# Two-part F32R queries and keys, two heads stacked in the halves of the TensorE array, and maxima units of two PSUM banks

## The chip, the cores and the metric

The kernel runs on one core of one Trainium2 chip. The metric is the device time of one execution in microseconds, from the first instruction to the last. It is given as the median of three runs. A profile of one more execution is read beside it. The core's engines are PE (TensorE, the matrix array), DVE (VectorE), ACT (ScalarE), POOL (GpSimd) and SP (SyncE, which here only issues transfers). Each works through its own stream of instructions in order, and they meet at semaphores.

## The reference

Two batches of 2048 tokens of 256 numbers pass one attention layer with 16 heads of 16 dimensions and then a feed-forward layer with eight experts and a shared one. Each is added to its input and normalised.

```python
q_mat = split_heads(x @ Wq.T + bq)
k_mat = split_heads(x @ Wv.T + bv)
v_mat = split_heads(x @ Wk.T + bk)
q_mat, k_mat = _xpos_rotate(q_mat, k_mat)      # rotation and a scale by position
scores = jnp.einsum('bhqd,bhkd->bhqk', q_mat, k_mat) / math.sqrt(DH * NUM_HEADS)
scores = jnp.where(causal[None, None], scores, -jnp.inf)
weights = jax.nn.softmax(scores, axis=-1)
inter = jnp.einsum('bhqk,bhkd->bhqd', weights, v_mat)
...
return inter @ Wo.T + bo
...
x = _layernorm(x + attention(x)); x = _layernorm(x + experts(x))   # top 2 of 8, and the shared one
```

All inputs are 32-bit floats.

## The kernel before

The work falls into three stages.

*Projection.* 32 tiles of 128 tokens. For each, PE forms queries, keys and values (`project`, L547 and L554, plain 32-bit), DVE adds the biases (L853, L857), POOL multiplies by cosine and, with neighbours swapped, by sine (L1106, L1115), DVE adds the two (L864). A query or key is then split into three bf16 parts whose sum keeps its precision: ACT rounds to part 0 (L751), DVE subtracts (L868), ACT rounds to part 1 (L755), DVE subtracts to part 2 (L873). PE transposes the twelve 128x128 pieces (`turn_parts`, L566), ACT copies them out (L762), and every four tiles SP stores them to a scratch tensor in device memory (L1158).

*Attention.* The 16 heads of two batches make eight groups of four heads. For a group SP loads a stack of queries and a stack of keys (`load_stack`, L1174): 96 partitions hold six products of parts (`Q_PARTS`, `K_PARTS`) times 16 dimensions, so that one product of 96 rows sums them. Three more rows hold ones on the key side and, on the query side, the negative row maximum in three bf16 parts (L1177, L1188). There are three pairs of stacks. The staging buffers of the projection are the memory of stack 1.

The maxima come first: for a block of 512 queries, PE forms scores with queries on the PSUM partitions (`max`, L584, after a product with the causal mask on the diagonal, L582), one bank of up to 512 columns a unit. Four banks take turns. DVE reduces each (L879). When a block's units are done, DVE makes the shift (`shift`, L887 to L901), PE transposes it (`shift_rows`, L596), ACT copies (L770), SP puts the rows into the stack. Then come the scores themselves, keys on the partitions (`score`, L616), in steps of one tile of 128 keys by one block of 512 queries for four heads. ACT takes the exponential (L779), POOL zeroes the masked triangle on diagonal tiles (L1126), and PE multiplies by the values with the four heads in four column tiles of 32 (`attend`, L633). A group has 40 steps: 28 of 512 columns and four each of 384, 256 and 128. Three banks take turns for scores, and a score waits for the exponential three places before (`score_ring`). PE and DVE turn and normalise a finished block of output (L645, L906, L909).

*Experts.* Products of F32R pairs (high and low part, L525 to L527), with ACT, DVE and POOL beside. This stage isn't touched.

One list, `plan.order`, sets every engine's order. Maxima units are produced by a generator, and `attend_all` draws from it at a pace: during the last steps of the projection two or three at each of three places, later after each score, by a debt (`owed`) that grows with the score's width and shrinks by the unit's cost. The maxima thus run ahead of the scores, by up to a group and more. `load_stack n + 2` is issued when group n starts, stacks 1 and 2 right after the projection. In group 7 preparatory work of the experts (output products, weight splitting) takes the maxima's place.

## Time and profile before

| | us |
|---|---|
| median of 3 runs (lowest, highest) | 1504.7 (1504.17, 1504.73) |
| the profiled execution, as a whole | 1507.14 |
| its span from first to last instruction | 1505.6 |
| PE busy in the span | 1369.6 |
| DVE busy | 1201.3 |
| ACT busy | 868.5 |
| POOL busy | 371.8 |
| mean granted TensorE clock | 0.967 of full |

A row of a timeline gives the start, the length and the instruction, `xN` for N of them in a run, and in brackets how long the engine was idle before and who released it. A matrix product's length reaches to its modelled end, while the next one may start long before; what a product costs in a dense stream is the distance between starts. PEld is the loading of weights. A 32-bit product is recorded as two passes.

### The profile page before, as it was taken

What the parts mean: (1) busy time and instruction counts of PE and PEld (TensorE: products, weight loads), DVE (VectorE), ACT (ScalarE), POOL (GpSimd) and SP (SyncE); (2) the same over time, 40 slices, a digit from 0 to 9 for tenths busy, and PEclk for the clock granted to TensorE, in tenths of its full rate; (3) what the DMA queues carried; (4) which work ended last, traced back from release to release, by engine and by line L of the source; (5) the groups of instructions that cost most, each with busy time, mean ns of one, the idle gap of its engine ahead of it and who ended that gap; (6) DMA issues with size and microseconds to landing.
All of it is one profiled execution on the core that took longest, in us unless ns stands there. A gap on an engine that the chain in (4) does not pass through costs nothing.

```text
span 1505.6 us, 23890 instructions
## 1 busy us (share of the span) xinstructions
PE 1369.6 (91%) x8656; PEld 707.3 (47%) x8656; DVE 1201.3 (80%) x2438; ACT 868.5 (58%) x1686; POOL 371.8 (25%) x708
## 2 busy tenths in 40 slices
PE   6677685799999999999999999998989999999997
PEld 3444331333333333333333333333436888888886
DVE  6998995598888888888888888887865677667766
ACT  2554343466776776777776776776764344434443
POOL 8775410111112112112112112112101322222222
PEclk9998978799999999999999999999989999999999
DMA  2338239103304205106006000002200000000000
GB/s 89 113 113 141 82 71 124 23 2 49 39 1 58 30 1 68 20 2 79 10 2 86 2 2 1 2 1 71 92 29 15 15 15 14 1 15 15 15 15 29
DMA packets 35589, 58.36 MB, mean 39 GB/s; under 512 B 3344, under 2 KB 26000, under 8 KB 35472
## 3 DMA queue, kind: packets, MB, share of 16 engines
q1 hardware_dynamic: 32576, 51.66, 19.1%
q10 hardware_dynamic: 2896, 5.18, 1.2%
q8 instruction: 69, 1.13, 0.3%
q14 instruction: 48, 0.39, 0.1%
HBM read 39.26 MB, written 16.78 MB: 37 GB/s over the span
## 4 chain that ended last, share of the span: by engine, by line
PE 73%; DVE 11%; DMA 5%; issue 5%; ACT 2%; SPq 2%; POOL 1%; ACTq 0%; POOLq 0%; DVEq 0%
PE psum L633 18%; PE psum L616 17%; PE psum L584 14%; PE psum L525 7%; PE psum L527 6%; PE psum L526 6%; DVE row_max L879 3%; DVE tokens L864 2%; DMA q_stack<-shift_t 2%; PE psum L582 2%; DVE tokens L868 2%; DMA k_stack<-ones 2%; SPq L1174 1%; PE psum L645 1%; DVE tokens L873 1%
## 5 line engine op out<-in xcount | busy, mean ns | idle before, releaser
L879 DVE TENSOR_REDUCE row_max<-psum 128x1 f32<-128x512 f32 (+3 forms) x1120 | 681.8, 668 | 132.4 <-PE psum L584 128.6
L779 ACT ACTIVATE probs<-psum 128x512 f32<-128x512 f32 (+3 forms) x1280 | 599.4, 535 | 266.3 <-PE psum L616 260.6
L616 PE MATMUL psum<-q_stack,k_stack 99*128 99x512 bf16 (+3 forms) x1280 | 427.2, 354 | 45.4 <-DMA q_stack<-shift_t 27.4
L584 PE MATMUL psum<-k_stack,q_stack 96*128 96x512 bf16 (+3 forms) x1280 | 419.5, 355 | 5.5 <-DVE row_max L879 5.3
L1126 POOL TENSOR_SCALAR_AFFINE_SELECT probs<-probs 128x128 f32<-128x128 f32 x512 | 146.3, 297 | 764.2 <-ACT probs L779 758.9
L633 PE MATMUL psum<-probs,v_aug 128*32 128x512 f32 (+3 forms) x2560 | 304.5, 547 | 0.0
L616 PEld LDWEIGHTS psum<-q_stack,k_stack 99*128 99x128 bf16 x1280 | 118.2, 98 | 360.7 <-ACT probs L779 224.7
L584 PEld LDWEIGHTS psum<-k_stack,q_stack 96*128 96x128 bf16 x1280 | 126.9, 100 | 106.2 <-DVE row_max L879 16.4
L1142 POOL TENSOR_TENSOR hid_low<-hidden,hid_high 128x512 fp32r<-128x512 f32 x72 | 93.1, 1293 | 298.4 <-ACT hid_high L838 259.4
L838 ACT CAST hid_high<-hidden 128x512 fp32r<-128x512 f32 x72 | 44.6, 619 | 122.0 <-DVE hidden L1036 122.0
L1052 DVE SCALAR_TENSOR_TENSOR tokens<-psum,combine,tokens 128x256 f32<-128x256 f32 x256 | 105.9, 476 | 2.0 <-PE psum L527 1.4
L582 PE MATMUL psum<-causal,ident 128*128 128x128 bf16 x512 | 101.9, 224 | 5.6 <-DMA k_stack<-ones 3.3
L633 PEld LDWEIGHTS psum<-probs,v_aug 128*32 128x32 f32 x2560 | 51.3, 108 | 95.8 <-ACT probs L779 43.8
L525 PE MATMUL psum<-w_down_high,hid_high 128*128 128x256 f32 x288 | 84.0, 292 | 8.5 <-POOL hid_low L1142 8.5
L527 PE MATMUL psum<-w_down_high,hid_low 128*128 128x256 f32 x288 | 83.0, 288 | 0.0
L526 PE MATMUL psum<-w_down_low,hid_high 128*128 128x256 f32 x288 | 82.8, 287 | 0.0
L832 ACT ACTIVATE silu<-psum 128x512 f32<-128x512 f32 x72 | 43.1, 599 | 63.9 <-PE psum L527 63.7
L1115 POOL TENSOR_TENSOR tokens<-tokens,rot_sin 128x256 f32<-128x256 f32 x64 | 77.3, 1228 | 0.0
L1036 DVE TENSOR_TENSOR hidden<-psum,silu 128x512 f32<-128x512 f32 x72 | 49.6, 689 | 34.5 <-PE psum L527 34.5
L547 PE MATMUL psum<-w_qkv,x_t 128*128 128x512 f32 x128 | 68.0, 657 | 9.7 <-DMA x_t<-x_t_dram 5.2
L566 PE MATMUL psum<-ident,tokens 128*128 128x128 bf16 x384 | 28.4, 227 | 45.9 <-DVE tokens L873 45.9
L582 PEld LDWEIGHTS psum<-causal,ident 128*128 128x128 bf16 x512 | 51.3, 100 | 28.8 <-DVE row_max L879 7.0
(120 smaller groups left out, 1657.2 us busy)
## 6 DMA issues: line engine op xcount, KB each, us to landing
k_stack<-parts_scratch SPq DMA_DIRECT2D x48, 256.0 KB, 9.6
q_stack<-parts_scratch SPq DMA_DIRECT2D x48, 256.0 KB, 20.2
parts_scratch<-q_stack SPq DMA_DIRECT2D x4, 1536.0 KB, 5.5
parts_scratch<-k_stack SPq DMA_DIRECT2D x4, 1536.0 KB, 5.5
x_res<-x_dram SPq DMA_DIRECT2D x8, 512.0 KB, 3.9
out_dram<-tokens SPq DMA_DIRECT2D x16, 256.0 KB, 2.2
x_t<-x_t_dram ACTq DMA_DIRECT2D x7, 512.0 KB, 3.7
q_stack<-shift_t SPq DMA_DIRECT2D x96, 4.0 KB
```

Of the source, the lines that this page charges most:

```text
L525: pe.matmul(out, lhs[0], rhs[0], start=first, stop=False)
L526: pe.matmul(out, lhs[0], rhs[1], start=False, stop=False)
L527: return pe.matmul(out, lhs[1], rhs[0], start=False, stop=last)
L582: pe.matmul(out[:, width - P:width], b.ident16[:], b.causal16[:], start=True, stop=False, skip_group_check=True)
L584: mm = pe.matmul(out, qs[0:SLOT_ROWS, first + j, i * P:(i + 1) * P], ks[0:SLOT_ROWS, first + j, kb * BLOCK:kb * BLOCK + width], start=kb < ...
L616: pe.matmul(bank(place % SCORE_BANKS)[:, off:BLOCK], b.k_stack[n % STACKS][0:SCORE_ROWS, j, kt * P:(kt + 1) * P], b.q_stack[n % STACKS][0: ...
L633: mm = pe.matmul(bank(3)[j * COL_TILE:(j + 1) * COL_TILE, off:BLOCK], b.v_aug[n // GROUPS][:, kt, col:col + COL_TILE], b.probs[step % 2 * ...
L779: act.activation(b.probs[step % 2 * GROUP + j][:, off:BLOCK], bank(place % SCORE_BANKS)[:, off:BLOCK], ACT.Exp, scale=SOFTMAX_SCALE).then_ ...
L879: dve.tensor_reduce(b.row_max[:, qb % 2, a, first:first + heads, kb], bank(4 + place % MAX_BANKS)[:, 0:heads * width].rearrange("p (h n) - ...
L1052: op = dve.scalar_tensor_tensor(out=b.tokens[:, i, :], in0=y, scalar=b.combine[blk % 2][:, pair * 2 + a, k - 1:k], in1=b.tokens[:, i, :], ...
L1126: pool.affine_select(out=pr[:, off:off + P], in_=pr[:, off:off + P], pattern=[[1, P]], compare_op=ALU.is_ge, fill=0.0, base=0, channel_mul ...
L1142: pool.tensor_tensor(b.hid_low[n % 2][:], b.hidden[n % 2][:], b.hid_high[n % 2][:], ALU.subtract).then_inc(s.h_low_made, 1)
```

## The change

Queries and keys are split into two parts of F32R, the rounded 32-bit type, in place of three of bf16. Three products of parts take the place of six, so a head needs 48 rows and, with two shift rows, 50. A stack holds two heads side by side, one in partitions 0 to 63, one from 64 (`SIDES`, `side_rows`), and a product for one head uses one half of the array's rows. Heads go in pairs: two scores follow each other, then maxima. A maxima unit covers both halves, with one PSUM bank for each, and DVE reduces both in one instruction; two such units take turns in the place of four single banks. The mask is added by four bf16 products on the halves. The even and odd dimensions of a head are permuted to lie in two runs of eight. In the projection the sine products move from POOL to DVE, and the subtraction that makes the second part moves to POOL; ACT rounds once; PE transposes eight 32-bit pieces. The scratch tensor holds 32-bit numbers. The rows of ones are loaded into each stack once only.

```diff
-PARTS = 3
+PARTS = 2
-Q_PARTS = (0, 0, 1, 1, 0, 2)
-K_PARTS = (0, 1, 0, 1, 2, 0)
+Q_PARTS = (0, 1, 0)
+K_PARTS = (0, 0, 1)
+SIDES = 2
+PAIRS = GROUP // SIDES
+ROW_TILE = P // SIDES
-MAX_BANKS = 4
-SHIFT_LAG = 8
+MAX_UNITS = 2
+SHIFT_LAG = 6
...
     def maxima_of(self, n, qb):
...
-                heads = 1 << (BLOCK // width).bit_length() - 1
-                for first in range(0, GROUP, heads):
+                pairs = min(PAIRS, BLOCK // width)
+                for first in range(0, PAIRS, pairs):
...
-                    yield heads * width + REDUCE_COST
+                    yield SIDES * pairs * width + REDUCE_COST
...
-            for j in range(GROUP):
-                self.score_ring.append(("exp_done", step * GROUP + j + 1))
...
-                owed += pace * (BLOCK - max(0, kt * P - qb * BLOCK))
+            for pair in range(PAIRS):
+                for j in range(pair * SIDES, (pair + 1) * SIDES):
+                    self.score_ring.append(("exp_done", step * GROUP + j + 1))
...
+                owed += pace * SIDES * (BLOCK - max(0, kt * P - qb * BLOCK))
                 while owed > 0:
                     owed -= next(side, BLOCK)
...
-            self.q_stack[i] = sbuf(f"q_stack{i}", [P, GROUP, SEQ], BF16, room, side)
+            self.q_stack[i] = sbuf(f"q_stack{i}", [P, PAIRS, SEQ], F32R, room, side)
...
         elif kind == "turn_parts":                       # PE
-                mm = pe.transpose(turned[:, n * P:(n + 1) * P],
-                                  b.qk_part[i % 4][:, n // 4, (n % 4) * P:(n % 4 + 1) * P], b.ident16[:])
+                mm = pe.transpose(bank(2, 2)[:, n * P:(n + 1) * P],
+                                  b.qk_part[i % 4][:, n // 4, (n % 4) * P:(n % 4 + 1) * P], b.ident[:])
...
         elif kind == "max":                              # PE
             if i == 0 and first == 0:
                 pe.wait_ge(s.stack_in[n % STACKS], stack_value(n))
...
+            units = [bank(4 + place % MAX_UNITS * SIDES + r)[:, 0:pairs * width] for r in range(SIDES)]
+            if kb == qb:
+                for half in range(2):
+                    for r in range(SIDES):
+                        rows = side_rows(r, ROW_TILE)
+                        pe.matmul(units[r].rearrange("p (n w) -> p n w", n=pairs)[:, :, width - P:width],
+                                  b.halves16[rows, half, :], b.causal16[rows, half, 0:pairs, :],
+                                  start=half == 0, stop=False, skip_group_check=True)
+            for pair in range(pairs):
+                for r in range(SIDES):
+                    rows = side_rows(r, SLOT_ROWS)
+                    mm = pe.matmul(units[r][:, pair * width:(pair + 1) * width],
+                                   qs[rows, first + pair, i * P:(i + 1) * P],
+                                   ks[rows, first + pair, kb * BLOCK:kb * BLOCK + width],
+                                   start=kb < qb, stop=True, skip_group_check=True)
...
         elif kind == "score":                            # PE
-                      b.k_stack[n % STACKS][0:SCORE_ROWS, j, kt * P:(kt + 1) * P],
-                      b.q_stack[n % STACKS][0:SCORE_ROWS, j, qb * BLOCK + off:(qb + 1) * BLOCK],
+                      b.k_stack[n % STACKS][side_rows(j, SCORE_ROWS), j // SIDES, kt * P:(kt + 1) * P],
+                      b.q_stack[n % STACKS][side_rows(j, SCORE_ROWS), j // SIDES, qb * BLOCK + off:(qb + 1) * BLOCK],
...
         if kind == "bias":                               # DVE
+            for e in range(2):
+                dve.tensor_tensor(
+                    swp5[:, :, :, e, :], raw5[:, :, :, 1 - e, :],
+                    sin4[:, :, e, :].unsqueeze(2).to_broadcast([P, 2, HEADS, DH // 2]), ALU.mult
+                ).then_inc(s.swapped, 1)
...
-        elif kind == "split":
-            dve.tensor_tensor(b.qk_rot[i % 4], b.qk_rot[i % 4], b.qk_part[i % 4][:, 0, :], ALU.subtract
-        elif kind == "split_last":
-            dve.tensor_tensor(b.qk_part[i % 4][:, 2, :], b.qk_rot[i % 4], b.qk_part[i % 4][:, 1, :], ALU.subtract
         elif kind == "max":                              # DVE
             dve.tensor_reduce(
-                b.row_max[:, qb % 2, a, first:first + heads, kb],
-                bank(4 + place % MAX_BANKS)[:, 0:heads * width].rearrange("p (h n) -> p h n", h=heads),
+                b.row_max[:, qb % 2, a, :, first:first + pairs, kb],
+                units[:, :, 0:pairs * width].rearrange("p r (h n) -> p r h n", h=pairs),
                 AX.X, ALU.max).then_inc(s.max_read, 1)
...
+        elif kind == "split":                            # POOL
+            pool.tensor_tensor(part[:, 1, :], b.qk_rot[i % 4], part[:, 0, :], ALU.subtract).then_inc(s.low_made, 1)
...
         elif kind == "load_stack":                       # SP
+                    for r in range(SIDES):
+                        row = r * ROW_TILE + slot * DH
+                        sp.dma_start(dst[row:row + DH, :, :].bitcast(F32),
+                                     src.rearrange("(h r d) n -> r d h n", r=SIDES, d=DH)[r]
+                                     ).then_inc(s.stack_in[n % STACKS], DMA)
```

The order of PE in a full step of a steady group, before. L616 is a score product, L584 a maxima product, L633 the probabilities by the values; 128x512 are output partitions and columns.

```order
L616 MATMUL psum<-q_stack1,k_stack1 128x512
L584 MATMUL psum<-k_stack2,q_stack2 128x512
L616 MATMUL psum<-q_stack1,k_stack1 128x512
L584 MATMUL psum<-k_stack2,q_stack2 128x512
L616 MATMUL psum<-q_stack1,k_stack1 128x512
L584 MATMUL psum<-k_stack2,q_stack2 128x512
L616 MATMUL psum<-q_stack1,k_stack1 128x512
L584 MATMUL psum<-k_stack2,q_stack2 128x512
L633 MATMUL psum<-probs0,v_aug1 32x512
```

The same place now. L634 is a score, L601 a maxima product (two make a unit), L651 the probabilities by the values.

```order
L634 MATMUL psum<-q_stack2,k_stack2 128x512 x2
L601 MATMUL psum<-k_stack0,q_stack0 128x512 x2
L634 MATMUL psum<-q_stack2,k_stack2 128x512 x2
L601 MATMUL psum<-k_stack0,q_stack0 128x512 x2
L651 MATMUL psum<-probs0,v_aug0 32x512
L651 MATMUL psum<-probs1,v_aug0 32x512
```

Scores and maxima alternated one by one and now alternate two by two; the number of products in a step is the same.

PE where it first needs stack 1 (`k_stack1`), in the fifth step of group 0. Before, the first product with `k_stack1` stood in the twentieth step.

```order
L651 MATMUL psum<-probs0,v_aug0 32x384
L651 MATMUL psum<-probs1,v_aug0 32x384
L651 MATMUL psum<-probs2,v_aug0 32x384
L651 MATMUL psum<-probs3,v_aug0 32x384
L634 MATMUL psum<-q_stack0,k_stack0 128x128 x2
L595 MATMUL psum<-causal16,halves16 128x256 x4
L601 MATMUL psum<-k_stack1,q_stack1 128x128 x4
L634 MATMUL psum<-q_stack0,k_stack0 128x128 x2
```

At the projection's end 66 of group 0's 72 units stand in the order now, where it was 70 of 140. The first unit of group 1 moved ahead to the fifth step.

DVE for one tile of the projection before (the last row begins the next tile): two bias additions, then rotation sum and two subtractions.

```order
L853 TENSOR_TENSOR tokens<-psum,b_qkv 128x512
L857 TENSOR_TENSOR v_aug<-psum,b_qkv 128x16x16
L864 TENSOR_TENSOR tokens<-tokens 128x512
L868 TENSOR_TENSOR tokens<-tokens 128x512
L873 TENSOR_TENSOR tokens<-tokens 128x512
L853 TENSOR_TENSOR tokens<-psum,b_qkv 128x512
```

DVE for one tile now: two bias additions, two sine products of half the width, the rotation sum.

```order
L874 TENSOR_TENSOR tokens<-psum,b_qkv 128x512
L878 TENSOR_TENSOR v_aug<-psum,b_qkv 128x16x16
L890 TENSOR_TENSOR tokens<-tokens,rot_sin 128x32x8 x2
L898 TENSOR_TENSOR tokens<-tokens 128x512
L874 TENSOR_TENSOR tokens<-psum,b_qkv 128x512
```

Two operations of 512 columns went and two of 256 came.

## Rows read from the trace of the kernel before

**Rows 1.** Busy time by stage: length, busy us (PE, PEld, DVE, ACT, POOL), clock.

```profile
140.25:212.00 71.75, 50.97 (x276) 27.67 (x276) 66.32 (x111) 23.27 (x26) 19.87 (x18) 0.82 0.18 63
361.60:1021.20 659.60, 648.95 (x4441) 239.99 (x4439) 561.64 (x1051) 469.52 (x1009) 108.67 (x384) 1.00 0.21 26
1021.20:1145.90 124.70, 110.96 (x734) 47.90 (x732) 89.88 (x230) 82.66 (x173) 19.41 (x64) 0.95 0.20 62
```

**Rows 2.** Timeline (start, length, engine) of one full step: PE, ACT, DVE.

```profile
236.32 0.39 PE L616 MATMUL psum<-q_stack,k_stack 99*128 99x512 bf16 x1
...
237.85 0.38 PE L616 MATMUL psum<-q_stack,k_stack 99*128 99x512 bf16 x1
...
238.38 1.06 PE L633 MATMUL psum<-probs,v_aug 128*32 128x512 f32 x8
239.38 0.39 PE L616 MATMUL psum<-q_stack,k_stack 99*128 99x512 bf16 x1
...
236.75 2.12 ACT L779 ACTIVATE probs<-psum 128x512 f32<-128x512 f32 x4 [1.00 <-PE psum L616]
...
235.71 4.34 DVE L879 TENSOR_REDUCE row_max<-psum 128x1 f32<-128x512 f32 x7
```

**Rows 3.** Timeline of one projection tile, and one operation with POOL quiet.

```profile
50.39 0.68 DVE L853 TENSOR_TENSOR tokens<-psum,b_qkv 128x512 f32<-128x512 f32 x1
51.32 1.65 DVE L864 TENSOR_TENSOR tokens<-tokens 128x512 f32<-128x512 f32 x1
...
55.39 0.68 DVE L853 TENSOR_TENSOR tokens<-psum,b_qkv 128x512 f32<-128x512 f32 x1
...
51.20 1.94 PE L547 MATMUL psum<-w_qkv,x_t 128*128 128x512 f32 x4
...
51.15 1.27 POOL L1106 TENSOR_TENSOR tokens<-tokens,rot_cos 128x512 f32<-128x512 f32 x1 [1.23 <-DVE tokens L853]
...
195.33 0.68 DVE L868 TENSOR_TENSOR tokens<-tokens 128x512 f32<-128x512 f32 x1
```

**Rows 4.** Timeline of the expert stage: F32R weight loads, F32R products of 512 columns.

```profile
1299.99 0.19 PEld L527 LDWEIGHTS psum<-w_down_high,hid_low 128*128 128x128 f32 x1
1300.10 0.19 PEld L525 LDWEIGHTS psum<-w_down_high,hid_high 128*128 128x128 f32 x1
...
1300.82 0.39 PE L526 MATMUL psum<-x_low,w_gate_high 128*128 128x512 f32 x1
1301.05 0.39 PE L527 MATMUL psum<-x_high,w_gate_low 128*128 128x512 f32 x1
```

**Rows 5.** Timeline: stores, stack loads, and PE's waits for them.

```profile
102.84 0.36 SPq L1158 DMA_DIRECT2D parts_scratch<-k_stack  x1
108.42 2.71 SPq L1174 DMA_DIRECT2D k_stack<-parts_scratch  x6
140.24 0.29 PE L582 MATMUL psum<-causal,ident 128*128 128x128 bf16 x1 [3.33 <-DMA k_stack<-ones]
...
217.59 2.67 SPq L1174 DMA_DIRECT2D k_stack<-parts_scratch  x6
273.19 0.29 PE L616 MATMUL psum<-q_stack,k_stack 99*128 99x128 bf16 x1 [27.38 <-DMA q_stack<-shift_t]
```

**Rows 6.** Groups by shape over the whole span: busy, mean ns of one, idle before.

```profile
L879 DVE TENSOR_REDUCE row_max<-psum 128x1 f32<-128x512 f32 x896 | 563.2, 683 | 109.3 <-PE psum L584 106.0 <-PE psum L616 0.3
L879 DVE TENSOR_REDUCE row_max<-psum 128x1 f32<-128x384 f32 x128 | 64.4, 549 | 7.6 <-PE psum L584 7.2
L779 ACT ACTIVATE probs<-psum 128x512 f32<-128x512 f32 x896 | 474.9, 598 | 183.6 <-PE psum L616 181.1
L779 ACT ACTIVATE probs<-psum 128x128 f32<-128x128 f32 x128 | 28.2, 277 | 51.3 <-PE psum L616 51.1
```

**Rows 7.** Timeline: four narrow scores on three banks.

```profile
802.70 0.34 PE L616 MATMUL psum<-q_stack,k_stack 99*128 99x128 bf16 x3
...
803.30 0.23 PE L616 MATMUL psum<-q_stack,k_stack 99*128 99x128 bf16 x1
```

232 lines of the change are left out of this document (113 added, 119 removed).

## The prediction

> **What bounds the kernel now.** I read the busy table by stage first. The span has four stages: projection (0 to 212 us), the first attention group with a long hole in it (212 to 361.6), six steady groups (361.6 to 1021.2, 109.9 each) and a last one (124.7), and from 1145.9 the expert stage, which the change doesn't touch. In a steady group PE is busy 108.2 us, DVE 93.6, ACT 78.3 [rows 1]. PE's busy time holds pipelined ends, so I read its timeline next. One full step runs from 236.32 to 239.38, 3.06 us: the fourth score product starts at 1.53, and by 2.06 nine products (four scores, five maxima) have passed, 0.22 each with 0.09 of a mode change; then the eight records of probabilities by values take 1.00 until the next score product starts. No wait stands in it; ACT had 1.00 idle before its four exponentials [rows 2]. So a steady group is bound by PE's own stream. With four maxima products a step would be 2.84; I take 3.0 as the mean of the 28 full steps, which leaves (109.9 - 84)/4 = 6.5 us for each block's three narrow steps, turning and shift rows.
>
> The projection is bound by DVE: 5.00 us from one tile's bias to the next (50.39 to 55.39) with no idle: two PSUM operations start the next after 0.60 and 0.33, and three SBUF operations share the other 4.07, 1.36 each [rows 3]. From 140.24 the maxima join, 61 units before the last tile is copied out at 212.0. Then PE stands still for 27.4 us, to 273.19, until shift rows land that queue behind 24 stack loads [rows 5].
>
> **Part 1, projection to 212.** DVE loses two of its three 512-wide SBUF operations and gains two of 256 (the swaps, from POOL). Beside a busy POOL a 512-wide one takes 1.36 (the row shown is 1.65 long), with POOL quiet 0.68 [rows 3]. DVE per tile: 0.93 + two such widths, 1.4 to 2.7 = 2.3 to 3.6. POOL: 1.27 (cosine) + as much again for a subtraction of the same size [rows 3] = 2.6. PE: four passes in 1.94, 0.43 each without the last one's tail [rows 3], = 1.73, half of that for the values, and eight 32-bit transposes, which I put at the spacing of 32-bit weight loads, 0.11 to 0.12 [rows 4]: 1.0. PE at 3.6 plus a mode change is the longest: 3.8 a tile (bounds 3.4 and 4.6), against 5.0.
>
> That gain isn't kept, because the maxima wait for stack 0. Tile 15 is turned in the 19th step: 11 + 18 x 3.8 = 79, plus 4.6 for products, transposes and copy = 84. The store took 5.6 us for 1.5 MB (102.84 to 108.42), 7.4 for 2 MB; the stack's 3.1 MB took 31.8 from first issue (108.42) to the first maxima at 140.24, and the bytes per stack don't change [rows 5]: 123. The maxima are due at 11 + 25 x 3.8 = 106, so PE stands for 17 us. From 123: seven tiles at 3.1 of DVE = 22, and 57 units ahead of the last copy. A reduction of 512 starts the next after 0.607 (7 in 4.34, of which the last counts 0.68 [rows 2]); 128 more elements cost 0.134 (683 against 549 ns [rows 6]), so a two-bank unit of 1024 costs 0.607 + 0.536 = 1.14. The 57 units hold 107 times 512 elements: 107 x 0.536 + 57 x 0.07 = 61. 123 + 22 + 61 + 5 for dependencies (the same sum for before gives 67 of its 71.8) = 211. **Term: -1** (-12 to +15). But by then more maxima are done: 57 units of group 0's 72, where before it was 61 of 140.
>
> **Part 2, 212 to group 1.** Before, the rows of blocks 0 and 1 were sent ahead of the loads, and block 2's rows waited for both stacks. Now block 2's rows go ahead too, but group 1's first maximum, which needs stack 1, stands only four steps after the start (the piece of the order with k_stack1, in the section on the change), and whatever follows in PE's stream waits behind it: scores, probabilities by values, then ACT and DVE. Both loads with their rows took from 217.59 to 273.19, 55.6 us [rows 5], one 27.8. With 7.4 for the store, PE resumes 35 us after the last copy, at 246. The last rows of group 0 land at about 275 and are wanted 20 steps later, at 297: hidden. Then steps 4 to 39: DVE has 80 units with 150 x 512 elements, 150 x 0.536 + 80 x 0.07 = 86, plus about 9 for shifts and normalising = 95; PE by Part 3 about the same. 246 + 96 = 342 against 361.6. **Term: -18** beside the -1 (-35 to 0).
>
> **Part 3, six steady groups.** The order now is two scores, one maxima unit (two products), two scores, one unit, then probabilities by values. If the two halves run together, a pair costs one stream: F32R of 512 columns starts every 0.23, and its weight loads, 0.19 long, can start 0.11 to 0.12 apart [rows 4]. I take 0.24 a pair. Streams alone would be 4 x 0.24 + 1.09 = 2.05. But there are three score banks. A score's exponential starts 0.43 after it and takes 0.60 (236.32 to 236.75 [rows 2], 598 ns [rows 6]), and the next score to that bank starts 0.06 later: the narrow step shows it, 802.70 to 803.30 is 0.60, for an exponential of 277 ns [rows 6, 7]. Before, the fourth score came at 1.53 anyway. Now it would come at 0.48 and must wait for the first exponential, to 1.09; its maxima pair ends at 1.56, then 0.09 and 1.00: **2.65 a step**. ACT then works 2.06 of it, DVE 2 x 1.14 = 2.3. A group: 28 x 2.65 + 4 x 6.5 + 2 (32-bit weight loads of 0.12 in the narrow steps; transposes that now stand between half-array products) = 102.2, against 109.9. DVE by itself: 67 units with about 126 x 512: 67.5 + 4.7 + 8 = 80; ACT 78. Six groups: **-46**. Bounds: no less than DVE's and ACT's 80 with a little friction, 90 (-120); and 115 if the halves don't overlap (+31, below).
>
> This trace has no row halves, only the four column tiles of the value products, eight records in 1.06 us [rows 2]. The Trainium skill, "TensorE: Matmul & The Clock Gate", section "Measured speedup vs the span model", gives 3.07 times for four row tiles, not 4; no row here shows it. By it a pair would be nearer 0.28 than 0.24, and the time some 10 us longer.
>
> **Part 4, the last group** (124.7). Its PE stream mixes in 128-row products and transposes, so each step gains mode changes of about 0.1 while two score pairs save 0.4 and the bank wait takes most back. **Term: -1** (-12 to +10). The expert stage: 0; it starts from the same state.
>
> **Sum** against the profiled execution's span of 1505.6: -1 - 18 - 46 - 1 = -66, 1439.6. That execution took 1507.1 as a whole, the median of the runs 1504.7, so the span is within 1 us of it: 1504.7 - 66 = **1439**.
>
> **Rivals.**
> - *The halves run one after the other.* Then the step is 8 x 0.235 = 1.88, 0.09 and 1.00: 2.97 at best, 3.08 with the friction that before has, and narrow products are held to the load spacing of 0.12, and there are 96 mask products a group for 64: +5 a group, my estimate. Stage 2 still gains some 5. 1504.7 + 6 x 5 + 8 - 5 = 1538, slower. It decides from a pair spacing over about 0.40. For it: no row halves are in the trace. Against: four column tiles do run together, reading 128 partitions each. 12 in 100.
> - *The bank wait costs little*, so that DVE and ACT bound a group at 90 to 94: -96 to -120 in Part 3, 1375 on the middle. For it: ACT is idle 1.00 a step now. Against: the chain score, exponential, score of 1.09 is a latency that a faster PE only exposes. 13 in 100.
> - *Waits multiply*: with two double units for four single banks, a DVE shift or normalising step (about 1 us) stops PE in its maxima and so the scores: 0.25 a step more, 2.9, so 1485. For it: one ring place is now 1.14 long. Against: the step leaves DVE 0.35 idle. 10 in 100.
> - *A half's next weight load waits for its running product.* A pair then costs 0.19 of load and 0.21 of stream, 0.40: unit at 0.40, third score at 0.80, fourth at 1.1, unit done by 1.75, step 2.85 to 2.9. A group is 28 x 2.9 + 28 = 109, so Part 3 gives -5 and Part 2 some -13: 1485. Against: loads of 0.19 us start 0.11 apart, beside running 128-row products [rows 4]. 5 in 100. The Trainium skill, "TensorE: Matmul & The Clock Gate", section "The mechanism", states this rule (a load overlaps a running product only in another row group); the trace disagrees with it for whole-array products.
> - *The clock.* While maxima and projection alternated, PE waiting often, the granted clock was 0.82 [rows 1]. If it dropped to 1.2 GHz for a good part of the groups, the value products alone would add up to 1.0 a step; 1550 and more. 4 in 100.
>
> Forecast: 56 in 100, with a range of its own of 1410 to 1465. For 8 in 10 the range is 1390 to 1500. A measurement of this kernel tells 0.2% (3 us) from no change. Faster: forecast 0.56, second rival 0.13, and 0.13 of the 0.15 of third and fourth = 0.82; within 0.2%: 0.03; slower: first and last rival with the rest, rounded, 0.15.
>
> **What would show it.** Projection: 3.8 us between biases, the first maxima at 123. A stop of PE of about 25 us at group 1's first maximum, ended by a load into k_stack or q_stack, and none at shift rows. In a group: score and maxima products in pairs whose starts lie within 0.02 us, the fourth score 1.09 after the first, ended by ACT; steps of 2.65; groups of 102. Were pairs 0.23 apart, the first rival holds; were the steps 2.3 to 2.4, the second. I would be wrong on the whole if the groups stayed at 110, or if stack loads of longer rows ran at another rate than 3.1 MB in 28 us.

## The result: 5% slower, and the profile after

The changed kernel takes 1585.6 us (median of four runs, 1574.4 to 1616.1), and the kernel before 1504.7. The ratio is 1.0514, 95% interval [1.0435, 1.0592]. Ratios, here and below, leave out executions over 1.5% above the fastest of the same kernel, while the medians hold all (here the one of 1616.1 is left out). I had predicted 1439, with 1390 to 1500 as range: wrong in sign. The profiled execution took 1574.41 as a whole (span 1573.2) at a mean clock of 0.944 (before 0.967). The times of the other three follow their clocks: 1578.7 at 0.941, 1592.6 at 0.931, 1616.1 at 0.911.

The same marks as in [rows 1] divide it: the fourth store of parts, the last parts copied out (the eighth store is issued), the start of group 1, of group 7, and the first expert product. All in us of each span:

| stretch | before | predicted | measured |
|---|---|---|---|
| to the fourth store | 102.8 | 84 | 90.4 |
| fourth store to last parts copied | 109.2 | 127 | 177.2 |
| group 0 | 149.6 | 131 | 148.3 |
| groups 1 to 6 | 659.6 | 613 | 657.9 |
| group 7 | 124.7 | 124 | 133.7 |
| experts | 359.6 | 360 | 365.7 |
| span | 1505.6 | 1439.6 | 1573.2 |

The busy times by stage after, with the columns of [rows 1] (length; busy and count of PE, PEld, DVE, ACT, POOL; clock, DMA share, GB/s):

```profile
0.00:90.40 90.40, 74.05 (x282) 43.27 (x283) 75.58 (x96) 26.38 (x34) 57.11 (x57) 0.96 0.35 125
90.40:127.00 36.60, 18.19 (x79) 10.98 (x77) 23.90 (x28) 8.29 (x12) 15.21 (x12) 0.82 0.96 158
127.00:267.60 140.60, 88.70 (x378) 48.23 (x378) 97.82 (x108) 18.42 (x23) 23.88 (x18) 0.69 0.14 50
267.60:415.90 148.30, 116.52 (x844) 50.28 (x846) 109.98 (x119) 77.21 (x168) 18.22 (x64) 0.87 0.41 59
415.90:1073.80 657.90, 604.20 (x4500) 255.24 (x4496) 486.78 (x518) 462.81 (x1009) 108.98 (x384) 1.00 0.20 26
1073.80:1207.50 133.70, 117.83 (x733) 50.75 (x725) 86.97 (x174) 81.34 (x172) 20.94 (x65) 0.92 0.17 54
```

Three things are to be seen. The projection without maxima is faster (the fourth store at 90.4 us for 102.8, and 4.24 from one bias to the next for 5.00). With maxima beside it (127 to 267.6), DVE is busy only 97.8 of 140.6 and PE 88.7, at a clock of 0.69: each waits for the other. In the six steady groups PE's busy time fell by 45 and DVE's by 75 against [rows 1], and the length by less than 2.

PE's timeline at its two long stops, which are for a load of `x_t` (not foreseen) and for stack 1 (foreseen). That load of `x_t` is issued on ACT's queue at 101.6, while stack 0's loads run, and lands at 129.4, 27.7 us later; the four just before it took 3.4 to 3.8:

```profile
129.41 2.08 PE L557 MATMUL psum<-w_qkv,x_t 128*128 128x512 f32 x2 [19.07 <-DMA x_t<-x_t_dram]
...
305.09 0.61 PE L595 MATMUL psum<-causal,halves 64*128 64x256 bf16 x4 [18.09 <-DMA k_stack<-ones]
```

One full step with two maxima units, the counterpart of [rows 2], in PE's, PEld's and ACT's timelines:

```profile
510.68 0.50 PE L634 MATMUL psum<-q_stack,k_stack 50*128 50x512 f32 x2
511.02 0.39 PE L601 MATMUL psum<-k_stack,q_stack 48*128 48x512 f32 x2
511.25 0.39 PE L634 MATMUL psum<-q_stack,k_stack 50*128 50x512 f32 x1
511.86 0.50 PE L634 MATMUL psum<-q_stack,k_stack 50*128 50x512 f32 x1 [0.22 <-ACT probs L793]
511.86 0.72 PE L601 MATMUL psum<-k_stack,q_stack 48*128 48x512 f32 x2
512.52 1.06 PE L651 MATMUL psum<-probs,v_aug 128*32 128x512 f32 x8
513.51 0.50 PE L634 MATMUL psum<-q_stack,k_stack 50*128 50x512 f32 x2
...
510.79 0.19 PEld L601 LDWEIGHTS psum<-k_stack,q_stack 48*128 48x128 f32 x2
...
511.86 0.18 PEld L634 LDWEIGHTS psum<-q_stack,k_stack 50*128 50x128 f32 x1 [0.65 <-ACT probs L793]
...
511.21 2.07 ACT L793 ACTIVATE probs<-psum 128x512 f32<-128x512 f32 x4 [0.77 <-PE psum L634]
```

The first row is a pair (x2) in 0.50 us, its two starts 0.003 apart: both halves run at once, as predicted. But the step is 2.83, not 2.65. The fourth score comes at 1.18 (predicted 1.09), and the value products, which stand behind its maxima pair, start 0.66 after it. Over the steady groups, steps with four maxima products and no mask have a median of 2.84 (72 of them), against 2.85 before (48). Over all 168 full steps the mean is 2.95 after and 2.99 before.

The first row answers to [rows 6]. A two-bank reduction is 1.22 long; where they follow each other without idle time they start 1.16 apart (median of 173; 1.14 predicted), and single ones before 0.60 apart. The other two rows are POOL's subtraction and DVE's sine products in the projection.

```profile
L904 DVE TENSOR_REDUCE row_max<-psum 128x2 f32<-128x1024 f32 x448 | 537.3, 1223 | 173.0 <-PE psum L601 168.2 <-PE psum L634 2.4
L1132 POOL TENSOR_TENSOR tokens<-tokens 128x512 fp32r<-128x512 f32 x32 | 46.0, 1439 | 9.9 <-ACT tokens L769 9.9
L890 DVE TENSOR_TENSOR tokens<-tokens,rot_sin 128x256 f32<-128x256 f32 x64 | 85.3, 1371 | 0.0
```

### The profile page after: what moved, and what is told of

It is laid out like the page before. It is cut to its first block, busy times and chain, and to the rows that moved or that the text cites. A ratio compares the mean times of both kernels' runs of the same rounds, so it can differ in the third digit from the quotient of the medians.

```text
span 1573.2 us, 23534 instructions
## 1 busy us (share of the span) xinstructions
PE 1364.2 (87%) x8784; PEld 750.8 (48%) x8784; DVE 1138.0 (72%) x1791; ACT 824.3 (52%) x1659; POOL 347.0 (22%) x685
## 4 chain that ended last, share of the span: by engine, by line
PE 58%; DVE 15%; issue 12%; ACT 7%; DMA 4%; POOL 3%; SPq 0%; POOLq 0%; DVEq 0%
PE psum L651 17%; PE psum L634 15%; ACT probs L793 7%; PE psum L601 7%; DVE row_max L904 6%; DVE tokens L890 5%; PE psum L535 4%; PE psum L537 4%; PE psum L536 4%; PE psum L557 2%; POOL hid_low L1156 2%; DMA x_t<-x_t_dram 2%; PE psum L595 2%; DMA k_stack<-ones 1%; DVE tokens L898 1%
## 5 line engine op out<-in xcount | busy, mean ns | idle before, releaser
L904 DVE TENSOR_REDUCE row_max<-psum 128x2 f32<-128x1024 f32 (+2 forms) x576 | 655.1, 1164 | 241.0 <-PE psum L601 234.0
L634 PE MATMUL psum<-q_stack,k_stack 50*128 50x512 f32 (+3 forms) x1280 | 387.3, 447 | 64.9 <-ACT probs L793 53.8
L634 PEld LDWEIGHTS psum<-q_stack,k_stack 50*128 50x128 f32 x1280 | 168.8, 186 | 407.8 <-ACT probs L793 325.1
L601 PE MATMUL psum<-k_stack,q_stack 48*128 48x512 f32 (+3 forms) x1280 | 317.6, 427 | 41.3 <-DVE row_max L904 40.7
L651 PE MATMUL psum<-probs,v_aug 128*32 128x512 f32 (+3 forms) x2560 | 305.7, 550 | 0.0
L601 PEld LDWEIGHTS psum<-k_stack,q_stack 48*128 48x128 f32 x1280 | 149.9, 194 | 64.9 <-DVE row_max L904 61.5
L595 PE MATMUL psum<-causal,halves 64*128 64x128 bf16 (+1 forms) x768 | 83.0, 246 | 34.2 <-DMA k_stack<-ones 18.1
L557 PE MATMUL psum<-w_qkv,x_t 128*128 128x512 f32 x128 | 78.6, 745 | 37.2 <-DMA x_t<-x_t_dram 23.4
L651 PEld LDWEIGHTS psum<-probs,v_aug 128*32 128x32 f32 x2560 | 51.0, 109 | 82.3 <-ACT probs L793 36.6
L890 DVE TENSOR_TENSOR tokens<-tokens,rot_sin 128x256 f32<-128x256 f32 x64 | 85.3, 1371 | 0.0
L769 ACT CAST tokens<-tokens 128x512 fp32r<-128x512 f32 x32 | 19.8, 618 | 118.3 <-DVE tokens L898 118.3
L1123 POOL TENSOR_TENSOR tokens<-tokens,rot_cos 128x512 f32<-128x512 f32 x32 | 40.6, 1269 | 141.7 <-DVE tokens L874 141.7
(118 smaller groups left out, 1573.2 us busy)
```

The lines of the kernel that those rows point to most:

```text
L595: pe.matmul(units[r].rearrange("p (n w) -> p n w", n=pairs)[:, :, width - P:width], b.halves16[rows, half, :], b.causal16[rows, half, 0:pa ...
L601: mm = pe.matmul(units[r][:, pair * width:(pair + 1) * width], qs[rows, first + pair, i * P:(i + 1) * P], ks[rows, first + pair, kb * BLOC ...
L634: pe.matmul(bank(place % SCORE_BANKS)[:, off:BLOCK], b.k_stack[n % STACKS][side_rows(j, SCORE_ROWS), j // SIDES, kt * P:(kt + 1) * P], b.q ...
L651: mm = pe.matmul(bank(3)[j * COL_TILE:(j + 1) * COL_TILE, off:BLOCK], b.v_aug[n // GROUPS][:, kt, col:col + COL_TILE], b.probs[step % 2 * ...
L890: dve.tensor_tensor(swp5[:, :, :, e, :], raw5[:, :, :, 1 - e, :], sin4[:, :, e, :].unsqueeze(2).to_broadcast([P, 2, HEADS, DH // 2]), ALU.mult
L904: dve.tensor_reduce(b.row_max[:, qb % 2, a, :, first:first + pairs, kb], units[:, :, 0:pairs * width].rearrange("p r (h n) -> p r h n", h= ...
```

## The experiments

Times are medians; a ratio is to the kernel before, run on the same chip. "Half clock" is the time at the lower level, 1.2 GHz, in the profiled execution, to which stretches, steps and rows belong. In diffs, `...` stands for what is left out.

### Where the projection's 68 us went

**e1_draw.** Half as many units drawn beside the projection.

```diff
-SIDE_STEPS = 2
-DRAIN_STEPS = 3
+SIDE_STEPS = 1
+DRAIN_STEPS = 2
```

> The changed kernel with half as many maxima units drawn during the projection (SIDE_STEPS 1 in place of 2, DRAIN_STEPS 2 in place of 3: 39 units instead of 66, as many elements as the kernel before reduced there). Theory A (the lost 56 us at the projection's end come from the two-unit ring met by DVE's in-order stream: each further pair of units in a tile adds a round trip between PE and DVE, at half clock): the last copy comes at 205 to 225 instead of 268, the 27 units come back in group 0 at no more than 15 us, the whole is 1535 to 1550. Rival B (those 56 us are the units' own DVE time, brought forward): the projection ends 30 us earlier but the units cost the same later, the whole stays within 10 us of 1580.

Measured: the last parts are copied at 215.2, 52 us earlier. Group 0 took 154.2, groups 111 each, group 7 155.0 with 82 at half clock; 1587.7 us in all (1558.6 to 1603.3). The draws are counted in units, and the change doubled a unit: 66 of group 0's 72 units were drawn beside the projection, where before it was 70 of 140. Taking it back moves the last copy by 52 of the 56 us, and group 0 pays 6 of them back. That is as Theory A's numbers have it, though not its cause, the ring (e7_single). In this kernel's whole time the gain isn't shown, as its runs overlap those of the changed kernel (1574.4 to 1616.1); e4_both shows it.

**e7_single.** The changed kernel, each unit's two banks taken and reduced one by one (four ring places again).

```diff
-            dve.wait_ge(s.max_done, u + 1)
-            dve.tensor_reduce(... units[:, :, 0:pairs * width] ...)
+            for r in range(SIDES):
+                dve.wait_ge(s.max_done, SIDES * u + r + 1)
+                dve.tensor_reduce(... units[:, r, 0:pairs * width] ...)
```

> The changed kernel with the two-bank units undone: each half's bank is a ring place of its own, waited for, reduced and freed by itself (1152 reductions of at most 512 in place of 576 of at most 1024; four places in place of two). Everything else as changed. Theory A (the ring of two places is what makes the projection's end serial): the last copy comes before 245 instead of 268; in the groups PE's step stays 2.83, DVE works 2.4 of it; the whole is 20 us or more below 1580. Rival B (the order of the draws and the clock make it serial, whatever the ring): the last copy stays within 8 us of 268, and the whole within 10 or above.

Measured: last copy at 268.9 (267.6), groups 108.4 to 111.3, 1612.9 us, ratio 1.0639 [1.0563, 1.0716]. The ring of two double places is thus the cause neither of the late copy nor of the groups' length.

**e5_xt3.** e4_both (below) with a third buffer for `x_t`, whose load is requested one block earlier.

```diff
-        self.x_t = [sbuf(f"x_t{i}", [P, CHUNKS, BLOCK], F32, proj) for i in range(2)]
+        self.x_t = [sbuf(f"x_t{i}", [P, CHUNKS, BLOCK], F32, proj) for i in range(3)]
```

> The kernel of the fourth run (half the draws, second draw ahead of the fourth score) with three buffers for the transposed tokens, so that each block of four tiles is requested one block earlier. In the changed kernel PE waited 19.1 us for such a block at 110 to 129 us, behind the twelve stack loads. Theory A (that wait is a transfer queued behind the stack, and it is on the path): the wait goes, the last copy comes 12 to 19 us earlier than 214.6, the whole is about 1512. Rival B (the first maxima wait for the same stack right behind it): the wait moves to the first mask product, and the whole stays within 5 us of 1528.

Measured: 1521.9 us, ratio 1.0106 [1.0074, 1.0137] (e4_both 1.0172); last copy at 207.5, 7 us earlier. The stop for `x_t` is gone. Of its 19 us 10.7 come back as a wait of the first maxima for stack 0 itself.

**e8_before_draws.** The kernel before, given what the change did to the draws.

```diff
-SIDE_STEPS = 2
-DRAIN_STEPS = 3
+SIDE_STEPS = 4
+DRAIN_STEPS = 5
```

> The kernel before with four draws for each two during the projection and five for three in its last steps: about 128 of its single-bank units by the end, as many elements as the changed kernel's 66. Theory A (bringing that much forward costs by itself, because it can't be had back in groups that PE's stream bounds): the last copy comes at 245 to 265 instead of 212, group 0 gets no more than 20 us shorter, the whole is 1520 to 1540. Rival B (single banks take the load without harm): last copy at 240 at most and the whole within 8 us of 1504.

Measured: 1533.3 us, ratio 1.019 [1.017, 1.0209]. The last copy moves from 212.0 to 249.0, and only 14 us come back by group 7. So the early draws cost by themselves, in the old format too. The half clock grew with them, from 100 to 154 us, and how much of the 28 us is the clock's isn't separated. **e11_before_fewer** and **e12_before_none** go the other way (SIDE_STEPS, DRAIN_STEPS 1, 2 and 0, 0, the latter with EARLY_PACE 1.3 for 1.2):

> The kernel before with SIDE_STEPS 1 and DRAIN_STEPS 2 (40 single-bank units drawn beside the projection and not 70). Theory A (draws beside the projection cost more there than they save later, in either kernel): last copy stored at 185-200 us (212.0), group 0 155-160 (149.6), groups and the rest +0-5 in all; 1493-1502. Rival B: the old kernel stood at its best number of draws, and the time is 1504-1512.

> The kernel before with no maxima drawn beside the projection (SIDE_STEPS and DRAIN_STEPS 0, EARLY_PACE 1.3). Theory A: last copy at 170-185 us, group 0 160-170 us with no wait for stack 1, 1485-1500 in all; then the changed kernel's best schedule and the old one's are compared alike (e10_none_beside minus this one is what the edit itself is worth). Rival B: VectorE binds group 0 with 217 units in it, and it takes 1505-1520.

Measured: 1529.7 and 1536.1 us, both slower than before (ratios 1.0174 and 1.0209), against my expectation. The last copy came at 199.6 and 178.9, but group 0 took 185.8 and 206.8. PE's timeline in e12 says why: the stop for shift rows grew from 27.4 us (to 51.2 in e11).

```profile
241.22 0.29 PE L616 MATMUL psum<-q_stack,k_stack 99*128 99x128 bf16 x1 [49.48 <-DMA q_stack<-shift_t]
```

**e10_none_beside**, the same with the new format (on e9_pace, below):

> e9_pace with no maxima drawn beside the projection (SIDE_STEPS and DRAIN_STEPS 0, EARLY_PACE 1.3): 13 units stand before group 0, not 37. Theory A: the projection is bound by VectorE at 4.24 us a tile and is done at 165-180 us (207.5 in e5_xt3); 111 units then stand in group 0 and not 88, but group 1's first one comes late enough that stack 1 is there, so the wait of 10-18 us for it goes: group 0 takes 150-165 us, and the whole 1485-1505. Rival B: group 0 is bound by VectorE then (111 reductions of 1.1 us with 26 us of shift work, more than its 150 us) and takes what the projection gave back: 1510-1520.

Measured: last copy at 159.1, group 0 221.6 with a stop of 47.2 us for the same rows; 1555.2 us. My Theory A missed that the rows queue behind the loads however early these start. The next experiment follows from that.

### The loads ahead of the shift rows

**e13_before_stack2_late.** The kernel before, with stack 2's twelve loads issued after the rows of group 0's last block.

```diff
-        self.add("load_stack", 2)
...
             while steps[min(step + 2, len(steps) - 1)][:2] not in self.rows_by:
                 next(maxima)
+            if not third and (0, BLOCKS - 1) in self.rows_by:
+                third = True
+                self.add("load_stack", 2)
```

> The kernel before with stack 2's 12 loads moved on SyncE's queue from ahead of group 0 to behind the shift rows of group 0's last block (score step 19). Theory A: TensorE's 27.4 us stop at 245.8 us there (for q_stack<-shift_t of block 2) is that block's rows standing behind 24 stack loads (62 us of transfers), of which half suffices, so the stop shrinks to 0-5 us and group 0 comes from 149.6 to 122-132 us; in all 1477-1490. Rival B: the engines are short of nothing else there but VectorE's maxima for the same rows, the stop only moves by 5-10 us: 1495-1500.

Measured: **1477.3 us, ratio 0.9817 [0.9801, 0.9833]**, the fastest of all. Group 0 takes 120.3 and not 149.6, and no other stretch moved by more than a microsecond. Its halves and the steady groups by busy time, columns as above:

```profile
211.40:271.70 60.30, 59.68 (x391) 23.06 (x389) 55.74 (x105) 39.13 (x87) 13.60 (x48) 0.91 0.53 81
271.70:331.70 60.00, 59.01 (x382) 20.99 (x381) 55.71 (x108) 40.73 (x81) 4.49 (x16) 1.00 0.46 55
331.70:991.40 659.70, 649.05 (x4442) 239.97 (x4439) 561.77 (x1051) 469.61 (x1009) 108.04 (x384) 1.00 0.21 26
```

PE is busy 118.7 of 120.3; the stop of 27.4 [rows 5] is gone whole. **e14_e5_stack2_late** and **e16_after_stack2_late** are the same edit in e5_xt3 and in the changed kernel.

> The same move of stack 2's loads in e5_xt3 (where group 0 took 157.2 us and TensorE stopped 17.0 us at 251.8 for the shift rows). Theory A: group 0 at 130-142 us; in all 1495-1508. Rival B: group 0 is bound by the half clock and by VectorE there, 150-157 us, in all 1513-1522.

> The same move of stack 2's loads in the changed kernel alone, where the stop in group 0 (18.1 us at 287.0) is for stack 1's own loads, which stand first anyway. Theory A: stack 1's landing comes earlier only by what it shares with stack 2, so 0-8 us less in group 0 (148.3), and the clock's swings (1574-1616) may cover it. Rival B: the two stacks share the DMA engines evenly, so stack 1 lands up to 30 us earlier and the stop goes: group 0 at 125-132.

Measured: e14 1494.1 us, ratio 0.9921 [0.9904, 0.9938], group 0 137.3 (157.2). e16 1610.4: group 0 148.2, unchanged, PE still stopped 17.9 us for stack 1, and half clock in two of the groups (65 and 34 us). So SP's queue lands stack 1 before stack 2, and in the changed kernel stack 1 itself is late: 66 of 72 units are done by then, and group 1's stand a few steps on.

### The step

**e2_order.** The changed kernel, with the second draw of maxima between the third and the fourth score.

```diff
-            for pair in range(PAIRS):
-                for j in range(pair * SIDES, (pair + 1) * SIDES):
-                    ...
-                owed += pace * SIDES * (BLOCK - max(0, kt * P - qb * BLOCK))
-                while owed > 0:
-                    owed -= next(side, BLOCK)
+            for j in range(GROUP):
+                ...
+                if j in (1, 2):
+                    owed += pace * SIDES * (BLOCK - max(0, kt * P - qb * BLOCK))
+                    while owed > 0:
+                        owed -= next(side, BLOCK)
```

> The changed kernel with the second maxima draw of a step moved from behind the fourth score to between the third and the fourth. Theory A (a full step is 2.83 us because the fourth score waits for the first exponential to 1.18 and the maxima pair then follows it): the pair fills the wait, the value products start at 1.5 instead of 1.84, a full step is 2.5 to 2.6, a group about 101 to 103 instead of 109.7, the whole 45 to 60 us shorter than the changed kernel. Rival B (DVE or ACT bound the step anyway): the fourth score or the maxima move and the step stays within 0.1 of 2.83; under 15 us.

Measured: 1552.9 us, ratio 1.032 [1.0277, 1.0362], which is some 30 us less than the changed kernel and not the 45 to 60 expected; the profiled execution (1578.1) has 79 us at half clock in group 0, for 38. Two groups without a fall of the clock take 103.5 and 103.2 (109.7). The step with four maxima products now has a median of 2.61. The same step in e15_e14_side, which has this order too (PE's timeline):

```profile
531.77 0.50 PE L636 MATMUL psum<-q_stack,k_stack 50*128 50x512 f32 x2
532.11 0.39 PE L603 MATMUL psum<-k_stack,q_stack 48*128 48x512 f32 x2
532.34 0.40 PE L636 MATMUL psum<-q_stack,k_stack 50*128 50x512 f32 x1
532.36 0.62 PE L603 MATMUL psum<-k_stack,q_stack 48*128 48x512 f32 x2
532.95 0.49 PE L636 MATMUL psum<-q_stack,k_stack 50*128 50x512 f32 x1
533.37 1.07 PE L653 MATMUL psum<-probs,v_aug 128*32 128x512 f32 x8
534.37 0.50 PE L636 MATMUL psum<-q_stack,k_stack 50*128 50x512 f32 x2
```

What bounds it is read best where nothing else stands in a step. Group 7 has such steps. Before, in PE's, PEld's and ACT's timeline:

```profile
1077.12 0.82 PE L616 MATMUL psum<-q_stack,k_stack 99*128 99x512 bf16 x3
1077.55 2.07 ACT L779 ACTIVATE probs<-psum 128x512 f32<-128x512 f32 x4 [1.03 <-PE psum L616]
1078.19 0.10 PEld L616 LDWEIGHTS psum<-q_stack,k_stack 99*128 99x128 bf16 x1 [0.75 <-ACT probs L779]
1078.20 0.39 PE L616 MATMUL psum<-q_stack,k_stack 99*128 99x512 bf16 x1 [0.26 <-ACT probs L779]
1078.52 1.07 PE L633 MATMUL psum<-probs,v_aug 128*32 128x512 f32 x8
1079.51 0.10 PEld L616 LDWEIGHTS psum<-q_stack,k_stack 99*128 99x128 bf16 x1 [0.84 <-ACT probs L779]
```

and after:

```profile
1156.82 0.73 PE L634 MATMUL psum<-q_stack,k_stack 50*128 50x512 f32 x3
1157.35 2.07 ACT L793 ACTIVATE probs<-psum 128x512 f32<-128x512 f32 x4 [0.71 <-PE psum L634]
1158.00 0.18 PEld L634 LDWEIGHTS psum<-q_stack,k_stack 50*128 50x128 f32 x1 [0.89 <-ACT probs L793]
1158.00 0.50 PE L634 MATMUL psum<-q_stack,k_stack 50*128 50x512 f32 x1 [0.46 <-ACT probs L793]
1158.43 1.06 PE L651 MATMUL psum<-probs,v_aug 128*32 128x512 f32 x8
1159.42 0.18 PEld L634 LDWEIGHTS psum<-q_stack,k_stack 50*128 50x128 f32 x2 [0.84 <-ACT probs L793]
```

Both are one loop through PE and ACT: a score to its exponential (0.43 before, 0.53 after), the exponential and the freed bank (0.64, 0.65), the score into that bank to the value products (0.32, 0.43), and these (1.0). The sums are 2.39 and 2.60. The pairs are not in the loop. The 32-bit product is, twice, with 0.10 more each time. Its weights take 0.18 to load and not 0.10, and at both places, the first score of a step (1159.42) and the one that waited (1158.00), this load begins only then. That the load makes up the 0.10 is my reading of the rows; no run changed it alone. So the plain step is 0.2 us *longer* after the change. With four maxima products beside, the kernel before reaches 2.82 in the mean by its stream (eight products, then the value products). The changed one reaches the same by the loop, as long as one pair stands in it between the fourth score and the value products. Put before the fourth score, that pair costs nothing (2.61, the loop to 0.01).

**e3_same_half.** The scores in head order 0, 2, 1, 3, so that neighbours share a half.

```diff
+HEAD_AT = (0, 2, 1, 3)
...
+            h = HEAD_AT[j]
-                      b.k_stack[n % STACKS][side_rows(j, SCORE_ROWS), j // SIDES, kt * P:(kt + 1) * P],
+                      b.k_stack[n % STACKS][side_rows(h, SCORE_ROWS), h // SIDES, kt * P:(kt + 1) * P],
```

> The changed kernel with the scores taken in head order 0, 2, 1, 3, so that two scores that follow each other lie in the same half of the array and can't run together; outputs go to the same places. Theory A (the overlap of score pairs is worth nothing in a step, because the bank wait at 1.18 sets it): second score at 0.23 to 0.34 instead of 0.01, fourth still at 1.18 or at most 0.05 later, the whole within 8 us. Rival B (the overlap is what PE's time hangs on): each of the two pairs costs 0.23 more, 2 x 0.23 x 34 x 8 = about 125 us slower; half of that if one pair alone counts.

Measured: groups at full clock 109.5 and 110.8, as in the changed kernel. In a step with four maxima products the second score now comes at 0.34, the fourth still at 1.18, and the median step is 2.84. The overlap of score pairs is thus worth nothing in the step: the loop's reading again. But the whole took 1688.2 us (ratio 1.1265). By that number alone Rival B's 125 us would seem near; the profiled execution has 184 us at half clock in groups 2, 4 and 5, which neither theory had.

**e17_e15_attend_early** and **e18_e13_attend_early.** In either format, the value products moved ahead of the fourth score, to fill its wait.

```diff
             for j in range(GROUP):
+                if j == 3 and step >= 1:
+                    self.attend(step - 1)
...
-            if step >= 1:
-                self.attend(step - 1)
```

> e15_e14_side with the previous step's attend products moved from behind the fourth score to ahead of it. The loop of a step now reads: first score, 0.53 us to its exponential, 0.60, the fourth score into the bank that frees (at 1.18), 0.43 to the attend products, 1.0 to the next step's first score, 2.60 in all without any maxima, two waits for a 32-bit product in it; in the kernel before 0.43, 0.60, 0.32 and 1.0 (2.40). Theory A (this loop bounds the step, not TensorE's issue or the halves): the attend products fill the wait for the bank, a step with maxima takes 2.4-2.6 us (ACT's four exponentials are 2.40) and not 2.83/2.65, six groups at 96-102 us each (107.9), group 7 and group 0 5-10 us less too; in all 1410-1450. Rival B: the attend products wait there for the last exponential of the step before, which the early place uncovers, so the step stays at 2.65-2.85: 1480-1500.

> The same move in e13_before_stack2_late, the kernel before's part format. Theory A: with four single-bank maxima its step is issue on TensorE: 4 scores and 4 maxima of 0.23 and 0.99 of attend products are 2.83 us, the 2.82 measured, so little comes back there (0-4 us a group, from steps with waits); 1455-1480, so e17 lies 20-60 us below it and the changed format is worth its cost only in this order. Rival B: both gain alike (the waits are the same in both), or neither.

Measured: 1635.0 us, ratio 1.0843 [1.0808, 1.0879], and 1484.1 us, 0.9856 [0.9839, 0.9873] (e13 0.9817). For the new format Theory A fell. PE's timeline of e17:

```profile
431.21 0.73 PE L636 MATMUL psum<-q_stack,k_stack 50*128 50x512 f32 x3
432.39 0.49 PE L636 MATMUL psum<-q_stack,k_stack 50*128 50x512 f32 x1 [0.45 <-ACT probs L796]
432.40 0.71 PE L603 MATMUL psum<-k_stack,q_stack 48*128 48x512 f32 x2
433.04 1.07 PE L653 MATMUL psum<-probs,v_aug 128*32 128x512 f32 x8
434.03 0.73 PE L636 MATMUL psum<-q_stack,k_stack 50*128 50x512 f32 x3
```

The fourth score now goes with the first two of the next step, three in a row, and the *third* waits for a bank, again at 1.18. With three banks for scores, one wait per step stays in both places tried for the value products (a fourth bank wasn't tried). The maxima pair is behind the waiting score again, so the step is back at 2.82. Rival B named another wait (the last exponential); the rows don't show it. The clock fell in every group besides (120 us at half clock in groups 5 and 6), in a profiled execution that is the slowest of the six (1682.9; the others 1612.1 to 1651.2). For the old format the step is as expected, 2.85 as before, but the whole lies above the expected 1455 to 1480, as group 7 takes 7 us more than in e13 and the six groups 6 more.

### Both edits to the schedule together, and the end of the kernel

**e4_both** is e1_draw with e2_order.

> Both edits of the first two runs. If the two causes are separate they add up: 1580 - 40 - 50 = about 1490, some 15 us under the kernel before. If moving maxima out of the projection only loads the groups, the sum falls short: with the shorter step DVE has 2.3 of 2.5 us to do and no room, and the whole stays over 1510.

Measured: 1528.6 us, ratio 1.0172 [1.0136, 1.0209]. Last copy 214.6, groups 107.7 to 109.0 but for the first (112.7, 12 of it at half clock), with the share of maxima that e1 leaves to them, experts 365.7. The expected 1490 wasn't reached, so the two gains don't add up in full; but against e2_order's 1552.9 fewer draws pay 24 us where the step has room for them.

**e6_share** (e5_xt3 with MAX_SHARE 0.84 for 0.7, so that group 7 has half the maxima):

> The kernel of the fifth run with MAX_SHARE 0.84 in place of 0.7, so that 12 units instead of 21 are left to the last group, as much work as the kernel before left there (22 of 1120 single-bank units). Theory A (the last group is 6 to 9 us longer and the expert stage 6 because the planner's cost of a group became exact, where it was 2% too high and put more of the work ahead): the last group falls to about 125, the expert stage to 360, the six groups gain 2 us each at most; 5 us or more below the fifth run. Rival B (the groups have no room on DVE): the six groups take it all back, within 3 us of the fifth run.

**e9_pace** (e5_xt3 with the planner's cost of a group times 169/166):

> e5_xt3 with the planner's cost of a group 1.8% too high again (factor 169/166), the slip that the kernel before had and the changed one mended. By the planner's own order 10 of the 20 attention turns-and-products work items stood behind the last scores before, 15 in the changed kernel, 11 here; at group 7's start 565 of the 576 units are drawn, not 555. Theory A: the experts stage's +6 us (359.7 to 365.7; e5_xt3 368.1) is these items, so it comes to 360-362 us, group 7 (with 10 units fewer, 11 us of VectorE) stays at 131-135, the six groups grow by 0.5 us each; in all 1512-1518. Rival B: the +6 comes from something else of the changed kernel (an exhausted bank order, the clock), then the experts stage stays at 365-368.

**e15_e14_side** (e14 with SIDE_PACE 1.14 for 0.98):

> e14 with SIDE_PACE 1.14 for 0.98, so that 10 of the attention's turns are left behind the last scores, as in the kernel before, and not 15. Theory A: experts stage 360 us and not 366-368, group 7 +0-3: 2-7 us less than e14. Rival B: group 7 grows by what the experts lose, or falls to the half clock (e9_pace: 51 us of it there): the same or 5-15 us more than e14.

Measured: 1536.0, 1536.4 and 1495.8 us. e6 left the experts at 365.7 and gave group 7 145.6, 58 of it at half clock: Theory A fell. e9 brought the experts to 359.7 and e15 to 357.8. So the 6 us there are the planner's. Its cost of a group was 1.8% too high before, which by accident left room beside group 7 for more of the attention's output products. The change mended the formula, and five of the plan's work items moved behind the last score (15 for 10; in the traces 96 of the 192 output products stand there, for 72). The whole gained nothing by it: group 7 takes 152.2 in e9 (51 at half clock) and 139.5 in e15, e9 is 14 us above e5_xt3, and e15 isn't below e14.

## Why the prediction was wrong

**Projection (Part 1, -1; measured +55.6).** The size of a tile was fair: 4.24 for 3.8. DVE is the longest there, not PE, as each of its two swaps of 256 columns cost 1.37 beside a busy POOL (two that ran with POOL quiet took 0.41), where I had priced each at half of 1.36; my bound was 3.6. That stack 0 gives the maxima their start held (123 predicted; the stop ended at 129.4, though it was for `x_t`, which landed with the same loads). The step that failed is "+ 5 for dependencies". I summed DVE's work to 83 us (61 of reductions, 22 of tiles) and took 5 of slack from the kernel before. It was 97.8 of work (63.3 and 34.6) and 43 of idle: one tile's DVE block of about 4.3 us and six double reductions alternate with PE's passes. The clock was at half for 99 of the 177 us (31 of 109 before); what it adds to the idle time isn't separated. PE waits up to 4.9 for a reduction there, and DVE for PE after it. My own sum had the units doubled and I let it pass as equal, since [rows 5] gave the last stretch's length for 61 single units. e1_draw and e8_before_draws show the doubled draw to be what makes the stretch long.

**Group 0 (Part 2, -18; measured -1).** The mechanism held: PE resumed 37 us after the last copy (35 predicted), at a load into `k_stack`. What followed, 110.8 us for 96, failed with Part 3: its 80 two-bank units (as many as predicted) stand up to four to a step, and steps with six or eight maxima products took about 3.5. The clock has little part in it: of group 0's 38 us at half clock, 34 lie before PE resumes at 305.1.

**Steady groups (Part 3, -46; measured -2).** Halves do overlap. The failed step is "Now it would come at 0.48 and must wait for the first exponential, to 1.09; its maxima pair ends at 1.56". I read the bank wait off bf16 rows [rows 2, 7], where a score's exponential starts 0.10 sooner after it. I also counted *spacings* (0.23 and 0.24) between the fourth score and the value products, where the measured way is 0.66 from a stream that had stopped. The terms: 1.18 for 1.09, 0.66 for 0.56 (0.47 and the mode change), 0.99 for 1.00: 2.83 for 2.65. And a comparison within my own text went wrong: I set 2.65, a step of four maxima products, against before's *mean* of 3.0, though I had 2.84 for the like step. Measured like with like, the mean went from 2.99 to 2.95. Where no wait precedes them, loads do hide: the maxima pair's weights are loaded at 510.79, while the score pair of the same halves runs from 510.68 to 511.18. (The Trainium skill, "TensorE: Matmul & The Clock Gate", section "The mechanism", has a sentence by which a load overlaps a running product only in another row group; these rows go against it, as in the prediction. The same section also allows a load that goes to the background weight buffer, which the rows don't contradict.) The groups' DVE and PE did get lighter (PE's busy by 45 us, DVE's by 75), off the path.

**Group 7 and experts (Part 4, -1 and 0; measured +9 and +6).** The step without maxima is 2.60 for 2.40, and the median step with a set of output products went from 2.91 to 3.51. I priced mode changes here but not the longer way through the 32-bit product. The experts' +6 is the plan's mended cost, an edit that I saw in the diff and priced at nothing.

**The clock** was a rival at 4 in 100. The median lies 11 us above the profiled execution, and the profiled one has 176 us at half clock where before had 100. All variants of the new format have more than that 100 (130 us in e15, 380 in e3, 530 in e17), and so has the old one in two of the three runs that move its draws (154 in e8, 147 in e12, but 103 in e11; in e13 it is 72). In the changed kernel 136 of the 176 us lie in the projection's second half and group 0, where PE waits. Why it falls in a whole steady group of one run and not of the next was not found.

What is the change worth, then? With the hole closed in both and the new format's draws, order, third `x_t` buffer and pace fitted as well, e15 takes 1495.8 and e13 1477.3. By stretch, e15 against e13 (profiled spans 1489.2, 1475.0): projection -5.0, group 0 +16.9 (50 us at half clock, for 10), six groups -11.5, group 7 +15.5, experts -1.8. So tuned, the new format loses 14 us by the profiles and 18 by the medians. How much of that is the clock's (130 us at half for 72) wasn't separated.

## What to carry to other kernels

Find the loop before pricing the stream: write down which product releases which engine and which buffer comes free, and ask whether the instruction made cheaper stands in it. Making products overlap helps only outside it, and their latency, which grew here, counts inside it. When a unit of work changes size, look at every counter that counts units. And look at what queues in front of a small transfer: moving twelve loads behind it gained 28 us in the old format, where the new one gained nothing.

## What the runs showed of the hardware

- Products on the two row halves, 48 or 50 rows of the 32-bit rounded type and 512 columns, start 0.00 to 0.01 us apart (after, 510.68); the pair behind a step's first starts 0.34 after it, and the next product 0.23 after that (511.02, 511.25).
- A product of the rounded 32-bit type that has waited is recorded as 0.50 long, one in a stream as 0.39; a bf16 one is 0.39 in both cases. ACT, its reader, starts 0.53 after the first score of a step, and 0.43 after a bf16 one.
- POOL's subtraction of 512 with a rounded output takes 1.44, its product of 512 without one 1.27. DVE's product of 256 in SBUF takes 1.37 beside a busy POOL and 0.41 with POOL quiet.
- DVE's reduction of two banks at once (2 x 512) starts the next after 1.16, one of a single bank after 0.60.
- A queue of 24 loads of 256 KB, in two stacks of 12, lands in order: the first stack's last load 28.5 to 31.3 us after its first issue. A 4 KB row issued behind both waits for both (issued at 238.1, PE resumed at 273.2 before). A 512 KB load on ACT's queue beside one such stack landed 27.7 us after issue, the four just before it after 3.4 to 3.8.
